# Attention's maxima by query tile and key tile for four heads at once, with the mask added by a 16-bit product

## The chip, the cores and the metric

The kernel runs on one core of a Trainium2 chip. Its engines are TensorE (PE; its weight loads are PEld in the profile), VectorE (DVE), ScalarE (ACT), GpSimd (POOL) and SyncE (SP), which issues most DMAs. The metric is the device time of one execution in microseconds (us), as the median of a few runs; lower is better.

## What is computed

Four steps one after the other on x of 4 x 1024 tokens x 128 numbers, each added to x behind a normalisation: attention, an expert layer, a message step, the expert layer again. The change is in the attention, which for 16 heads of 8 numbers is this:

```python
k = _layernorm((x @ Wk).reshape(b, t, h, s), kln_w, kln_b)   # q the same way
v = (x @ Wv).reshape(b, t, h, s)
dot = jnp.einsum('bqhs,bkhs->bhqk', q, k) * scale
dot = jnp.where(causal, dot, -jnp.inf)          # a query sees keys up to itself
attn = jax.nn.softmax(dot, axis=-1)
out = jnp.einsum('bhqk,bkhs->bqhs', attn, v).reshape(b, t, e)
return out @ Wo + bo
```

## The kernel before

A batch's 1024 tokens are 8 tiles of 128 (P). Heads go in groups of four (GROUP), four groups a batch, 16 groups in all. A head's 8 numbers are stacked to 32 rows (exact parts of both factors, and two rows for the shift), so that four heads fill 128 rows. `k_apart` holds the keys of a group with each head's 32 rows in a slab of its own and zeros elsewhere, so one product of all 128 rows gives one head's scores.

The softmax needs each query's largest allowed score first. So each group's scores are made twice:

- **Maxima.** Queries on the partitions, keys along the columns: `matmul(out, qT tile, k_apart[:, head, keys])` (L706), read by VectorE from PSUM. The causal mask matters only in the last 128 columns of a query tile's keys. VectorE adds a mask and takes the maximum in one fused instruction (L1239; the profile names it CUSTOM_DVE_ANT_0, and a short DVE_READ_ACCUMULATOR2_ANT brings its result), which writes the masked scores to a scratch tile. Where a row of keys has more than 512 columns, its first 512 are below the diagonal and take a plain reduction (L1237) into `first_max`.
- **Shift.** `shift` (L1244) takes the maxima of a half (four query tiles) with the sign turned into two spare rows of the stacked queries, `q_st`: for the high half joined with `first_max` first (L1250), then L1251 and L1252. TensorE transposes the queries again (`turn_shifted`, L710), into `qmT`, and the second scores come out less the maximum.
- **Scores.** Keys on the partitions, queries along the columns (L719). ScalarE takes the exponential out of PSUM into `a_prob` (L903), GpSimd clears what lies above the diagonal, and `weigh` (L723, its matmuls L739) multiplies by the values, four heads side by side in the array.

Work goes by **units**: one unit is one of six PSUM banks of 512 columns (`a_bank`, RINGS = 6), filled by TensorE and emptied by one other engine. TensorE fills unit n when unit n - 6 has been emptied, whoever empties it. Before, a maxima unit is one head's piece of the table MAX_PIECES: per head two units of 128 + 256 columns, two of 384 and six of 512, 40 a group.

The order is one generator, `sequence`, that all engines walk. It runs over the 40 score units of a group; behind score i stands the share of the 40 maxima units of the **next** group that are due by i (of 38 slots, i = 0 to 37), and at fixed i stand transposes, projections, normalisations and the weighs: behind 5 (key tiles 6 and 7 of the group before), 15, 20, 27, 32, 36 and 39. `turn_low`, which needs the low half's shift, is at 21; the shift of the high half at 37, and `turn_high` at 3 of the next group. So a group's maxima are made beside the scores of the group before, 15 times; the first group's are made alone, in the opening. Units with a diagonal tile are DVE's L1239; `spread` (SyncE's DMAs) lays out the keys, and KEYS_FROM says which maxima unit first reads their low and high half.

The causal mask `mask` is 128 x 512 in 16 bits, zero but for the last 128 columns, made by GpSimd in the setup.

## Time and profile before

| | us |
|---|---|
| median of 3 runs | 2802.59 (2801.55 to 2805.32) |
| the profiled execution | 2805.4 |
| its span | 2803.6 |
| mean granted TensorE clock | 0.972 of 2.4 GHz |
| attention with its opening | about the first 680 |
| expert layer, message step, expert layer | the rest |

The profile is of one execution. A row of the timeline is start, length, engine, line, operation, and tiles as output<-inputs; matmuls overlap, and their ends are modelled, so what a product costs TensorE in a stream is the distance between two starts. "PEld a <- DVE b: us, times" is TensorE's load for a that waited for VectorE's b. In rows of stretches each engine has its busy time with its count of instructions in brackets, then the granted clock (1.00 is 2.4 GHz), and DMA.

### The profile page before, as it was taken

How to read it: one execution, taken by the hardware profiler on the slowest of the kernel's cores; microseconds unless marked ns; L12 is line 12 of the kernel's file. 1: busy time of each engine (PE TensorE's matmuls, PEld its weight loads, DVE VectorE, ACT ScalarE, POOL GpSimd, SP SyncE). 2: the span in 40 equal slices, each digit the busy share in tenths (PEclk: the TensorE clock that was granted, in tenths of full speed). 3: DMA queues.
4: the chain of work that ended last, by engine and by line, in shares of the span. 5: the costliest groups of instructions: out<-in, count | busy, mean ns of one | idle time of the engine just before them, and what ended most of it. 6: DMA issues, size and time to landing. Idle time of an engine off the chain costs nothing. (4 is left out here: it accounts for less than half of the span.)

```text
span 2803.6 us, 54930 instructions
## 1 busy us (share of the span) xinstructions
PE 2600.8 (93%) x18814; PEld 1690.2 (60%) x18814; DVE 1769.6 (63%) x4095; ACT 1594.4 (57%) x2912; POOL 821.7 (29%) x1181
## 2 busy tenths in 40 slices
PE   6999999986689889999999999999999999996897
PEld 4566565653578755555556666555555565554786
DVE  7877777783656655556655556555566655546466
ACT  2776677775534455555555556665565555544343
POOL 4152524335154311111111111122121233313542
PEclk7999999998999899999999999999999999998998
DMA  5500000002334278888888888887888788874222
GB/s 110 87 16 12 16 16 16 13 19 83 96 113 135 66 176 198 195 195 200 193 197 195 196 195 192 195 187 186 191 192 194 187 204 204 205 183 178 60 84 86
DMA packets 193508, 383.24 MB, mean 137 GB/s; under 512 B 46305, under 2 KB 101738, under 8 KB 191882
## 3 DMA queue, kind: packets, MB, share of 16 engines
q1 hardware_dynamic: 184650, 362.55, 54.1%
q0 software_dynamic: 8640, 17.84, 1.8%
q8 instruction: 129, 2.11, 0.3%
q14 instruction: 89, 0.73, 0.1%
HBM read 38.10 MB, written 39.86 MB: 28 GB/s over the span
## 5 line engine op out<-in xcount | busy, mean ns | idle before, releaser
L3123 DVE STREAM_TRANSPOSE m_turned<-m_sig 128x1024 f32<-128x1024 f32 x512 | 613.7, 1228 | 419.8 <-ACT m_sig L2893 203.4
L2715 PE MATMUL m_v_ps<-m_sig,m_tok 128*64 128x512 f32 x2048 | 467.7, 598 | 0.0
L2728 PE MATMUL m_v_ps<-m_sigT,m_tok 128*64 128x256 f32 x4064 | 461.5, 380 | 2.9 <-DMA m_sigT<-m_turned 2.9
L2699 PE MATMUL m_f_ps<-m_swap,m_own 64*128 64x512 f32 x1536 | 424.7, 403 | 10.9 <-DMA m_swap<-m_own 8.1
L2699 PE MATMUL m_f_ps<-m_own,m_swap 64*128 64x512 f32 x1536 | 424.8, 403 | 0.0
L903 ACT ACTIVATE a_prob<-a_bank 128x512 f32<-128x512 f32 (+1 forms) x640 | 329.0, 567 | 167.7 <-PE a_bank L719 162.8
L2728 PEld LDWEIGHTS m_v_ps<-m_sigT,m_tok 128*64 128x64 f32 x4064 | 289.5, 137 | 197.9 <-issue 56.2
L2893 ACT ACTIVATE m_sig<-m_f_ps 128x1024 f32<-128x1024 f32 x256 | 248.4, 1023 | 236.3 <-issue 138.8
L2989 POOL TENSOR_TENSOR m_own<-m_uv,m_own 128x1024 fp32r<-128x1024 f32 x64 | 151.9, 2373 | 765.7 <-ACT m_own L2855 765.7
L2699 PEld LDWEIGHTS m_f_ps<-m_swap,m_own 64*128 64x128 f32 x1536 | 270.8, 186 | 93.4 <-issue 24.6
L2715 PEld LDWEIGHTS m_v_ps<-m_sig,m_tok 128*64 128x64 f32 x2048 | 135.6, 136 | 264.5 <-issue 264.1
L2879 ACT ACTIVATE m_sig<-m_f_ps 128x512 f32<-128x512 f32 x512 | 264.5, 603 | 45.7 <-PE m_f_ps L2699 44.0
L719 PE MATMUL a_bank<-a_qmT,k_apart 128*128 128x512 f32 (+3 forms) x768 | 265.8, 383 | 22.5 <-DVE a_maxima L1239 10.9
L706 PE MATMUL a_bank<-k_apart,a_qT 128*128 128x512 f32 (+3 forms) x768 | 265.2, 389 | 13.4 <-DVE a_maxima L1239 5.2
L2699 PEld LDWEIGHTS m_f_ps<-m_own,m_swap 64*128 64x128 f32 x1536 | 270.6, 186 | 5.2
L1239 DVE CUSTOM_DVE_ANT_0 a_masked_out<-a_bank,mask 128x128 f32<-128x128 f32 (+3 forms) x512 | 222.9, 485 | 54.3 <-PE a_bank L706 52.9
L719 PEld LDWEIGHTS a_bank<-a_qmT,k_apart 128*128 128x128 f32 x768 | 140.1, 193 | 132.5 <-issue 61.3
L2905 ACT CAST m_v1T_hi<-m_v_ps 128x256 fp32r<-128x256 f32 x128 | 47.8, 373 | 271.3 <-PE m_v_ps L2728 266.7
L1237 DVE TENSOR_REDUCE a_first_max<-a_bank 128x1 f32<-128x512 f32 x256 | 165.2, 684 | 49.6 <-PE a_bank L706 47.7
L3132 DVE TENSOR_TENSOR m_v1T_lo<-m_v_ps,m_v1T_hi 128x256 fp32r<-128x256 f32 x128 | 54.3, 424 | 201.6 <-ACT m_v1T_hi L2905 201.6
L706 PEld LDWEIGHTS a_bank<-k_apart,a_qT 128*128 128x128 f32 x768 | 144.1, 197 | 52.6 <-DVE a_maxima L1239 21.9
L1899 PE MATMUL f_y_ps<-f_w_down,f_innerT 128*128 x1136 | 153.4, 278 | 22.9 <-DVE f_raw L2309 15.7
(509 smaller groups left out, 4315.3 us busy)
## 6 DMA issues: line engine op xcount, KB each, us to landing
m_sigT<-m_turned SPq DMA_DIRECT2D x2042, 128.0 KB, 2.3
m_swap<-m_own SPq DMA_DIRECT2D x64, 256.0 KB, 3.3
f_t_rows<-f_sent_rows SPq DMA_DIRECT2D x142, 65.0 KB
f_sent_rows<-a_proj SPq DMA_DIRECT2D x34, 260.0 KB, 8.9
k_apart<-a_kT SPq DMA_DIRECT2D x128, 64.0 KB, 2.0
m_swap<-m_own SPq DMA_DIRECT2D x64, 128.0 KB, 3.2
f_h<-back_rows SPq DMA_DIRECT2D x8, 512.0 KB, 5.1
rows<-back_rows SPq DMA_DIRECT2D x6, 512.0 KB, 3.8
```

Source lines behind the costliest of these rows:

```text
L706: mm = pe.matmul(out[:, col:col + k1 - k0], qT[G % 2][:, qt * P:(qt + 1) * P], k_apart[G % 2][:, h, k0:k1], start=True, stop=True)
L719: mm = pe.matmul(out[:, col:col + q1 - q0], k_apart[G % 2][:, h, j * P:(j + 1) * P], qmT[G % 2][:, q0:q1], start=True, stop=True)
L903: act.activation(to[:, h, start:start + width], src[:, 0:width], ACT.Exp).then_inc(u.free(), 1)
L1237: ins = dve.tensor_reduce(first_max[:, qt % HALF_T, h:h + 1], scores, AX.X, ALU.max)
L1239: ins = dve.tensor_tensor_reduce(out=masked, in0=scores, in1=k["mask"][:, HALF - width:HALF], scale=1.0, scalar=MASKED, op0=ALU.add, op1=A ...
L1899: mm = pe.matmul(y_ps[:, 0:DIM], innerT[p][:, ib * P:(ib + 1) * P], w_down[:, ds(e * INTER + ib * DIM, DIM)], start=(ib == 0), stop=(ib == ...
L2699: mm = pe.matmul(f_ps[s][:, cols], tile_of(u[rows, :], j + s * SIDE), v[rows, cols], start=start, stop=stop)
L2715: mm = pe.matmul(v2_ps[h * RANK:(h + 1) * RANK, :], tok[p][:, 0, j + s * SIDE, :], sig[j % 2][s][:, h * HALF:(h + 1) * HALF], start=(j == ...
L2728: mm = pe.matmul(v1_ps[h * RANK:(h + 1) * RANK, g * 2 * P:(g + 1) * 2 * P], tok[p][:, 1, jj, :], sigT[g][:, :, 2 * h:2 * h + 2, jj, :].rea ...
L2879: ins = act.activation(sig[1][s][:, cols], f_ps[s][:, cols], ACT.Sigmoid)
L2893: act.activation(sig[j % 2][s][:, :], f_ps[s][:, :], ACT.Sigmoid).then_inc(sig_ready, 1)
L3123: dve.transpose(turned[g][:, :, q, :, :], sig[j % 2][s][:, :].rearrange("p (t j a) -> p j t a", j=4, a=STACK)).then_inc(turn_ready, 1)
```

## The change

A maxima unit is now one query tile by one key tile for all four heads: 128 columns for each head, 512 in all. There are 36 such pairs on and below the diagonal; the first, of query tile 0, is split into two units of two heads, so a group has 37 units. They stand in the order: query tiles 0 to 3 with their key tiles (11 units, and then the low shift), tiles 4 to 7 by key tiles 0 to 3 (16), tiles 4 to 7 by the high key tiles up to their own (10). Behind the product of a diagonal pair TensorE adds the mask into the same bank: a second product with a 16-bit identity as weights and the 128 x 128 mask, repeated for the heads, as the moving side. VectorE takes one plain reduction from 512 columns to 4 maxima (`maxima` for key tile 0, `tile_max` for the others); the fused instruction and its scratch tiles are gone. `shift` joins the key tiles' maxima with one small step for each key tile from 1 on: three for the low half, seven for the high one, each waiting for the one before it.

```diff
@@ setup, GpSimd
-            pool.wait_ge(ident_zero, 2)
+            pool.memset(k["ident16"][:, :], 0.0).then_inc(ident_zero, 1)
+            pool.wait_ge(ident_zero, 3)
+            pool.affine_select(out=k["ident16"][:, :], in_=k["ident16"][:, :], compare_op=ALU.not_equal, fill=1.0,
+                               base=0, pattern=[[-1, P]], channel_multiplier=1).then_inc(ident16_done, 1)
-            corner = k["mask"][:, HALF - P:HALF]
+            corner = k["mask"][:, :]
@@ attention, tables
-    SCORE_UNITS, MAX_UNITS = 40, 40
+    SCORE_UNITS, MAX_UNITS = 40, 37
-        MAX_PIECES = (((0, 0, P), (1, 0, 2 * P)), ((2, 0, 3 * P),), ((3, 0, HALF),), ((4, 0, HALF),), ((5, 0, HALF),),
-                      ((4, HALF, 5 * P), (5, HALF, 6 * P)), ((6, 0, HALF),), ((6, HALF, 7 * P),), ((7, 0, HALF),), ((7, HALF, SEQ),))
-        MAXES = [(pieces, (h + GROUP // 2) % GROUP) for pieces in MAX_PIECES for h in range(GROUP)]
+        MAXES = [(0, 0, 0, 2), (0, 0, 2, 2)]
+        MAXES += [(qt, kt, 0, GROUP) for qt in range(1, HALF_T) for kt in range(qt + 1)]
+        MAXES += [(qt, kt, 0, GROUP) for qt in range(HALF_T, TILES) for kt in range(HALF_T)]
+        MAXES += [(qt, kt, 0, GROUP) for qt in range(HALF_T, TILES) for kt in range(HALF_T, qt + 1)]
-        KEYS_FROM = (0, 20)
-        MAXES_LOW = 12
+        KEYS_FROM = (0, 27)
+        MAXES_LOW = 11
@@ TensorE, maxima_unit
-                for qt, k0, k1 in pieces:
-                    mm = pe.matmul(out[:, col:col + k1 - k0], qT[G % 2][:, qt * P:(qt + 1) * P], k_apart[G % 2][:, h, k0:k1], start=True, stop=True)
-                    col += k1 - k0
+                to = out[:, 0:heads * P].rearrange("p (h k) -> p h k", h=heads)
+                mm = pe.matmul(to, qT[G % 2][:, qt * P:(qt + 1) * P], k_apart[G % 2][:, h:h + heads, kt * P:(kt + 1) * P], start=True, stop=kt < qt)
+                if kt == qt:
+                    mm = pe.matmul(to, k["ident16"][:, :], k["mask"][:, :].unsqueeze(1).broadcast_to([P, heads, P]), start=False, stop=True)
@@ VectorE, maxima_unit
-                for qt, k0, k1 in pieces:
...
-                        ins = dve.tensor_reduce(first_max[:, qt % HALF_T, h:h + 1], scores, AX.X, ALU.max)
-                        continue
-                    ins = dve.tensor_tensor_reduce(out=masked, in0=scores, in1=k["mask"][:, HALF - width:HALF], scale=1.0,
-                                                   scalar=MASKED, op0=ALU.add, op1=ALU.max, accum_out=maxima[:, qt, h:h + 1])
+                at = maxima[:, qt, h:h + heads] if kt == 0 else tile_max[:, qt, kt - 1, h:h + heads]
+                ins = dve.tensor_reduce(at, src[:, 0:heads * P].rearrange("p (h k) -> p h k", h=heads), AX.X, ALU.max)
@@ VectorE, shift
-                if n:
-                    link(dve.tensor_tensor(maxima[:, mine, :], maxima[:, mine, :], first_max[:, :, :], ALU.max))
+                for kt in range(1, (n + 1) * HALF_T):
+                    upper = slice(max(kt, mine.start), mine.stop)
+                    link(dve.tensor_tensor(maxima[:, upper, :], maxima[:, upper, :], tile_max[:, upper, kt - 1, :], ALU.max))
```

TensorE's program in batch 0, group 3, from score 28 to the weigh behind score 32 (L719 is a score, L706 a maxima product, L671 a transpose, L739 a weigh). Before:

```order
L719 MATMUL a_bank<-a_qmT,k_apart 128x512
L706 MATMUL a_bank<-k_apart,a_qT 128x384
L719 MATMUL a_bank<-a_qmT,k_apart 128x512
L706 MATMUL a_bank<-k_apart,a_qT 128x384
L719 MATMUL a_bank<-a_qmT,k_apart 128x512
L706 MATMUL a_bank<-k_apart,a_qT 128x512
L719 MATMUL a_bank<-a_qmT,k_apart 128x512
L671 MATMUL a_bank<-ident,k_st 128x128 x4
L706 MATMUL a_bank<-k_apart,a_qT 128x512
L719 MATMUL a_bank<-a_qmT,k_apart 128x384
L706 MATMUL a_bank<-k_apart,a_qT 128x512
L739 MATMUL a_o_acc<-a_prob,v 32x128 x4
```

The same place now, from the maxima product behind score 28 to the last instruction ahead of that weigh; L723 is a score, L709 a maxima product, L711 the mask's product, L674 a transpose:

```order
L709 MATMUL a_bank<-k_apart,a_qT 128x512
L723 MATMUL a_bank<-a_qmT,k_apart 128x512
L709 MATMUL a_bank<-k_apart,a_qT 128x512
L711 MATMUL a_bank<-mask,ident 128x512
L723 MATMUL a_bank<-a_qmT,k_apart 128x512
L709 MATMUL a_bank<-k_apart,a_qT 128x512
L723 MATMUL a_bank<-a_qmT,k_apart 128x512
L674 MATMUL a_bank<-ident,k_st 128x128 x4
L709 MATMUL a_bank<-k_apart,a_qT 128x512
L723 MATMUL a_bank<-a_qmT,k_apart 128x384
L709 MATMUL a_bank<-k_apart,a_qT 128x512
L711 MATMUL a_bank<-mask,ident 128x512
```

The maxima products are all 512 wide, and a mask product stands behind two of them, one of the two right ahead of the weigh.

VectorE at the shift of a high half, before; the ISA rows are the fused reduction and its short second instruction:

```order
L1239 ISA a_masked_out,a_maxima<-a_bank,mask 128x512 [waits a_unit_free4,a_unit_full]
L1239 ISA a_maxima 128x1
L1239 ISA a_masked_out,a_maxima<-a_bank,mask 128x512 [waits a_unit_free1,a_unit_full]
L1239 ISA a_maxima 128x1
L1250 TENSOR_TENSOR a_maxima<-a_maxima,a_first_max 128x16 [waits a_unit_free5]
L1251 TENSOR_SCALAR q_st<-a_maxima 128x4x4 [waits a_link]
L1252 SCALAR_TENSOR_TENSOR q_st<-a_maxima,q_st 128x4x4 [waits a_link]
```

And now:

```order
L1231 TENSOR_REDUCE a_tile_max<-a_bank 128x4 [waits a_unit_full] x13
L1241 TENSOR_TENSOR a_maxima<-a_maxima,a_tile_max 128x16 [waits a_unit_free4]
L1241 TENSOR_TENSOR a_maxima<-a_maxima,a_tile_max 128x16 [waits a_link] x3
L1241 TENSOR_TENSOR a_maxima<-a_maxima,a_tile_max 128x12 [waits a_link]
L1241 TENSOR_TENSOR a_maxima<-a_maxima,a_tile_max 128x8 [waits a_link]
L1241 TENSOR_TENSOR a_maxima<-a_maxima,a_tile_max 128x4 [waits a_link]
L1243 TENSOR_SCALAR q_st<-a_maxima 128x4x4 [waits a_link]
L1244 SCALAR_TENSOR_TENSOR q_st<-a_maxima,q_st 128x4x4 [waits a_link]
```

One join has become seven, each waiting for the last.

## Rows read from the trace of the kernel before

**Rows 1.** The page, part 1: busy us (share) x instructions of each engine.
```profile
PE 2600.8 (93%) x18814; PEld 1690.2 (60%) x18814; DVE 1769.6 (63%) x4095; ACT 1594.4 (57%) x2912; POOL 821.7 (29%) x1181
```

**Rows 2.** Engines' busy time in stretches S2, S5, S7 of a group, and all seven's sum.
```profile
core 0: us, PE busy (x) PEld busy (x) DVE busy (x) ACT busy (x) POOL busy (x), PEclk, DMA share, GB/s
...
187.65:195.77 8.12, 7.78 (x42) 3.91 (x38) 7.02 (x19) 5.88 (x11) 3.75 (x9) 1.00 0.00 0
...
206.99:210.99 4.00, 4.00 (x34) 2.53 (x30) 2.94 (x7) 2.94 (x6) 0.78 (x2) 1.00 0.23 51
...
214.75:216.60 1.85, 1.85 (x20) 1.10 (x16) 1.01 (x4) 1.33 (x3) 0.00 (x0) 1.00 0.00 0
sum 33.25, PE 32.91 PEld 20.71 DVE 25.68 ACT 23.46 POOL 9.13; mean PE 4.70 PEld 2.96 DVE 3.67 ACT 3.35 POOL 1.30
```

**Rows 3.** TensorE in order of time in that group: start, length, instruction.
```profile
183.69 0.62 PE L706 MATMUL a_bank<-k_apart,a_qT 128*128 128x128 f32 x4
184.15 0.40 PE L719 MATMUL a_bank<-a_qmT,k_apart 128*128 128x512 f32 x1
...
188.47 0.40 PE L706 MATMUL a_bank<-k_apart,a_qT 128*128 128x512 f32 x1
188.70 0.40 PE L719 MATMUL a_bank<-a_qmT,k_apart 128*128 128x512 f32 x1
...
193.91 1.92 PE L739 MATMUL a_o_acc<-a_prob,v 128*32 128x512 f32 x16
...
208.60 0.60 PE L671 MATMUL a_bank<-ident,k_st 128*128 128x128 f32 x4
208.96 0.48 PE L706 MATMUL a_bank<-k_apart,a_qT 128*128 128x512 f32 x1
209.28 0.34 PE L719 MATMUL a_bank<-a_qmT,k_apart 128*128 128x384 f32 x1
209.45 0.40 PE L706 MATMUL a_bank<-k_apart,a_qT 128*128 128x512 f32 x1
209.78 1.28 PE L739 MATMUL a_o_acc<-a_prob,v 128*32 128x128 f32 x16
```

**Rows 4.** VectorE in order of time in the opening, columns as in rows 3.
```profile
54.75 0.28 DVE L1239 CUSTOM_DVE_ANT_0 a_masked_out<-a_bank,mask 128x128 f32<-128x128 f32 x1
...
55.30 0.29 DVE L1239 CUSTOM_DVE_ANT_0 a_masked_out<-a_bank,mask 128x128 f32<-128x128 f32 x1
...
60.79 0.55 DVE L1239 CUSTOM_DVE_ANT_0 a_masked_out<-a_bank,mask 128x384 f32<-128x384 f32 x1
...
61.27 2.48 DVE L1237 TENSOR_REDUCE a_first_max<-a_bank 128x1 f32<-128x512 f32 x4
63.66 0.68 DVE L1239 CUSTOM_DVE_ANT_0 a_masked_out<-a_bank,mask 128x512 f32<-128x512 f32 x1
...
64.27 0.68 DVE L1239 CUSTOM_DVE_ANT_0 a_masked_out<-a_bank,mask 128x512 f32<-128x512 f32 x1
...
66.22 0.17 DVE L1250 TENSOR_TENSOR a_maxima<-a_maxima,a_first_max 128x16 f32<-128x16 f32 x1
66.43 0.18 DVE L1251 TENSOR_SCALAR q_st<-a_maxima 128x16 fp32r<-128x16 f32 x1
```

**Rows 5.** Waits over 150 to 650 us: us in total, times, longest; first and last of eight.
```profile
PEld a_bank L719 <- DVE a_maxima L1239: 24.2, 40, 2.5
...
PE a_bank L706 <- DVE a_first_max L1237: 1.0, 4, 0.3
```

**Rows 6.** Groups of instructions by form, and one line's durations (min/median/max).
```profile
L739 PE MATMUL a_o_acc<-a_prob,v 128*32 128x512 f32 x768 | 99.2, 604 | 5.5 <-POOL a_prob L1049 4.1 <-ACT a_prob L903 1.4
...
L1237 DVE TENSOR_REDUCE a_first_max<-a_bank 128x1 f32<-128x512 f32 x256 | 165.2, 684 | 49.6 <-PE a_bank L706 47.7
...
L1172 DVE TENSOR_REDUCE a_qk_var<-a_spare x8: 895/1204/1218, 35.8 to 448.9; 128x128 f32<-128x1024 f32 x6, 128x96 f32<-128x768 f32 x2
```

**Rows 7.** Engines' busy time in the opening's maxima, columns as in rows 2.
```profile
42.50:66.80 24.30, 20.54 (x50) 12.41 (x49) 24.13 (x85) 0.59 (x1) 14.72 (x20) 0.62 1.20 189
```

More of the change, by code:

```diff
@@ L344, in attention_phase @@
     HEAD_STAGES, EARLY_UNITS = 5, 12
-    MASKED_OUTS = 2
     with ExitStack() as ctx, ExitStack() as phase:
@@ L368, in attention_phase @@
         qT, kT, qmT = ([sb(f"a_{n}{i}", [P, SEQ], F32R) for i in range(c)] for n, c in (("qT", 2), ("kT", 1), ("qmT", 2)))
-        maxima, first_max = sb("a_maxima", [P, TILES, GROUP]), sb("a_first_max", [P, HALF_T, GROUP])
-        masked_out = [sb(f"a_masked_out{i}", [P, HALF]) for i in range(MASKED_OUTS)]
+        maxima, tile_max = sb("a_maxima", [P, TILES, GROUP]), sb("a_tile_max", [P, TILES, TILES - 1, GROUP])
         oT = sb("a_oT", [P, SEQ])
@@ L699, in maxima_unit @@
             def maxima_unit(u, G, n, stacks=()):
-                pieces, h = MAXES[n]
-                out, col = u.next(), 0
+                qt, kt, h, heads = MAXES[n]
+                out = u.next()
                 u.wait_empty(pe, *stacks)
@@ L1220, in stack_first, with maxima_unit @@
                 dve.memset(qs[:, :, :, 3 * HD:3 * HD + 2], 0.0).then_inc(queries_ready, 1)
[L1222 to L1224 removed]
+            def maxima_unit(u, n):
+                qt, kt, h, heads = MAXES[n]
+                src = u.next()
                 u.wait_full(dve)
[L1226 to L1240 removed]
+                at = maxima[:, qt, h:h + heads] if kt == 0 else tile_max[:, qt, kt - 1, h:h + heads]
+                ins = dve.tensor_reduce(at, src[:, 0:heads * P].rearrange("p (h k) -> p h k", h=heads), AX.X, ALU.max)
                 ins.then_inc(u.free(), 1)
@@ L1443, in early_table, with group @@
                 dve.tensor_scalar(k["early_expert"][:, :], expert_sum[0:1, :], -1.0, None, ALU.add)
-            def group(u, link, b, g, prev, prep, follows, masked_by, head_made=()):
+            def group(u, link, b, g, prev, prep, follows, head_made=()):
                 ahead, projected = (g + 1) % GROUPS, []
@@ L1449, in group @@
                     if what == "max":
-                        made = maxima_unit(u, n, masked_by)
+                        made = maxima_unit(u, n)
                     elif what == "next_keys":
@@ L1531, in _ @@
             u.n += 4
-            masked_by = []
             for what, n in opening():
                 if what == "max":
-                    made = maxima_unit(u, n, masked_by)
+                    made = maxima_unit(u, n)
                 elif what == "shift":
@@ L1540, in _ @@
             u.next()
-            group(u, link, 0, 0, False, False, True, masked_by)
+            group(u, link, 0, 0, False, False, True)
             before, made = link.n, ()
@@ L1545, in _ @@
                 for g in (1, 2, 3):
-                    made = group(u, link, b, g, True, True, True, masked_by, made)
-                made = group(u, link, b + 1, 0, True, True, True, masked_by, made)
-                masked_by = [n - UNITS_BATCH for n in masked_by]
+                    made = group(u, link, b, g, True, True, True, made)
+                made = group(u, link, b + 1, 0, True, True, True, made)
                 before += link.n
@@ L1553, in _ @@
             for g in (1, 2, 3):
-                made = group(u, link, b, g, True, False, g < GROUPS - 1, masked_by, made)
+                made = group(u, link, b, g, True, False, g < GROUPS - 1, made)
             for n in range(HALVES_OF):
@@ L3401, in hybrid_kernel @@
         with ExitStack() as attention:
-            allocate(attention, k, {"mask": ([P, HALF], BF16),
+            allocate(attention, k, {"mask": ([P, P], BF16), "ident16": ([P, P], BF16),
                                     "w_qkv": ([P, 3 * DIM], F32), "w_o": ([P, DIM], F32),
```

14 lines of the change are left out of this document (1 added, 13 removed).

## The prediction

> **What bounds the kernel now.** I read the page first [rows 1]: TensorE is busy 93% of the span, VectorE 63%, ScalarE 57%. The change touches attention alone, which fills about the first 680 us, so the whole-span shares decide nothing. I then took one steady group (batch 0, group 3), from 183.35 to 216.60 us, and cut it at the ends of its products with the probabilities (weigh) into seven stretches, S1 to S7 [rows 2]. The reader should see in the sum TensorE at 32.91 us of 33.25, VectorE at 25.68, ScalarE at 23.46: three engines that share a ring of six PSUM banks, at full clock. A busy TensorE is not one at its peak, because ends of matmuls are modelled, so I went down to start-to-start times.
>
> Paces on TensorE [rows 3]: 512-column products start 0.232 us apart (188.47, 188.70), a 384-column one takes 0.175 (209.28 to 209.45), and two units of 128 plus 256 columns fill 183.69 to 184.15, 0.23 each. Transposes of four tiles take 0.36 (208.60 to 208.96), and the 512-column product right behind them 0.32 (208.96 to 209.28), 0.09 more than in the stream. Paces on VectorE [rows 4]: masked reduction of 512 columns 0.61 us, of 384 0.48, a pair 128 plus 256 0.555 (54.75, 55.30); four plain reductions of 512 take 2.39, so 0.598 each; a small step on the maxima 0.21.
>
> With these, S5 is 5 scores (4 x 0.232 + 0.175 = 1.10), 5 maxima units (3 x 0.232 + 2 x 0.175 = 1.05), one transposing unit 0.36 and weigh 1.21: 3.72 of its 4.00 us. The other 0.28 is what TensorE loses behind transposes and on either side of a weigh, 0.09 to 0.1 each (the weigh starts at 209.78, 0.33 after a product that wants 0.23 [rows 3]). So S5 is TensorE's, and so by the same count are S1, S3, S4, S6 and S7 (VectorE is busy 2.94 of 4.00 us in S5 [rows 2]). S2 is different: 10 scores 2.21, 11 units 2.44, weigh 1.9 (its row at 193.91 [rows 3]) make 6.5 of 8.12 us, and VectorE is busy for 7.02: VectorE sets that stretch by giving banks back late. Over 150 to 650 us TensorE's loads and matmuls of scores and maxima wait for VectorE's maxima in eight rows, from 24.2 down to 1.0 us, together 65 [rows 5].
>
> **The change part by part.** Maxima of a group are made 16 times: once in the opening, alone, and 15 times between the scores of the group before.
>
> TensorE, columns. Before, per group: 4 heads x (2 x 0.23 + 2 x 0.175 + 6 x 0.232) = 8.8 us. Now 35 units of 512 columns and 2 of 256 (two in 0.23): 8.35 us. Saved 0.4 us. The columns multiplied are the same; only the narrow pieces, which cost more per column, are gone.
>
> TensorE, masks. New are 9 identity products in 16 bits, 7 of 512 columns and 2 of 256. No row before has a 16-bit product. The nearest are products of the same shape in the same stream, 0.232 per 512 [rows 3]. Below: the weigh products, which run for four heads at once, 99.2 us for 768, 0.13 each [rows 6]. Above: the transposes, products with an identity too, 0.36 for 4 x 128 columns [rows 3]. I take 0.232, the row of equal shape: 8 x 0.232 = 1.86 us a group; the ends give 1.0 and 2.9.
> The Trainium skill (TensorE: Matmul & The Clock Gate, Back-to-back issue gap) states about 131 ns a matmul of 512 columns in a sustained stream of loads and matmuls. Rows 3 disagree with that (0.23); by it the masks would cost 8 x 0.131 = 1.05 us, and the sum below would be some 12 us smaller.
>
> Net on TensorE +1.4 us a group. Where it falls, with the units moved from 40 over 38 scores to 37 over 37: S1 +0.13, S2 +0.58 (two masks; the narrow units leave), S3 -0.23 (5 units for 6), S4 +0.35 (the mask of unit 27 and wider units), S5 +0.57 (masks of 29 and 32), S6 +0.23 (mask of 36), S7 -0.23 (no unit left). In S1 and S3 to S7 this is on the path: +0.82.
>
> VectorE, units. Before 4 x (2 x 0.555 + 2 x 0.48 + 6 x 0.61) = 22.9 us, now 35 x 0.598 + 2 x 0.35 = 21.6: it saves 1.3. This supposes that a reduction to four values costs what one to a single value does. The reduction of 1024 columns to 128 values lasts 1204 ns against 684 for 512 to one [rows 6]: 520 ns for 512 more columns, so outputs cost nothing; without that row 35 x 0.1 us would be at stake.
> The Trainium skill (VectorE: DVE Perf Modes, Rules for kernel authors) speaks against the change: `tensor_reduce` is "the slowest DVE op", to be restructured away. Rows 4 do not bear that out here (0.598 us between starts against 0.61 for the fused one); by the rule the units would cost more and the slower end of my range would be the likely one.
>
> VectorE, joins. The shift of the low half gets three more small steps, that of the high half six more: 9 x 0.21 = 1.9 us. The high ones run in S7, where VectorE has been idle beside the weighs (it is busy 1.01 of 1.85 us [rows 2]), and the transposes that need them come three scores into the next group; the last unit is now two scores earlier. They cost nothing there; without the cover 1.3 us a group. What is queued behind them is the next group's first unit, whose bank is needed six units later. The low ones run in S2, where VectorE sets the pace. S1 and S2 together on VectorE: units 9.63 to 9.07 us, shift +0.63, net +0.07. TensorE wants +0.58 in S2 and has 1.6 us of waits there to put it in. Bounds 0.07 and 0.58; I take 0.3, between, because a weigh needs the units before it issued, not averaged.
>
> Sum per group 0.82 + 0.3 = 1.12, times 15 = 16.8 us.
>
> Opening (42.5 to 66.8, VectorE busy 24.13 of 24.30 us, mean granted clock 0.62 [rows 7]). VectorE bounds it: 24.3 us before; now 21.6 of units, 1.5 for the low shift (0.89 + 0.63) and 2.0 for the high one (0.73 + 1.26): 25.1, +0.8. TensorE is mostly at its lower level there (1.2 GHz); twice 0.232 us, an estimate, for each of the last ten units and four masks is 6.5 us against VectorE's 6.0. The ring hides part of it; without that cover +0.5. Setup: GpSimd's 16-bit identity adds a memset and a selection, and the mask's memset shrinks to a quarter; VectorE waits for x, not for them. Nothing.
>
> Against the profiled run's own 2805.4 us the sum is +17.6: 2823.0. That run is 2.8 us over the median of 2802.6, so the forecast of the median is 2820. SyncE's spreads are not moved; the high keys are now first read at unit 27, not 20, later and not sooner.
>
> **Rivals.** A, slower by masks on the path: the sum above, 2820 (2811 to 2831).
> B, masks absorbed: TensorE's slack takes them. If the 0.28 us left in S5, and the like 0.56 in S4 and 0.36 in S6, could be filled, 1.2 us of a group's gain in work vanishes and 2803 to 2808 comes out. For it: waits for banks of 65 us. Against it: S5's slack is accounted for by what follows transposes and weighs, which a mask doesn't fill.
> C, masks dearer: 0.36 a mask instead of 0.232 adds 8 x 0.13 x 15 = 15 us: 2835; a loss of 0.09 us behind each 16-bit product, as behind transposes, adds 10 x 0.09 x 15 = 13: 2834; both, 2848.
> D, faster: VectorE's returning of banks, not TensorE, sets all stretches. Then each stretch goes by VectorE's own change: S1 -0.7, S2 +0.13, S3 -0.5, S4 +0.2, S5 +0.2, S6 -0.05, S7 -0.6 with the joins in idle time: -1.3 a group, 2784. It decides if TensorE's waits for banks in S3 to S7 are real and over 1 us a group. For it: the same 65 us. Against: VectorE is idle over 1 us of each stretch but S2.
> E, the change doesn't do what it says (units or masks other than 37 and 9 on the chip): its order lists them, so next to nothing.
>
> **Chances and range.** A 0.53, B 0.20, C 0.14, D 0.12, E 0.01. A measurement of this kernel can tell about 0.2%, 5.6 us, from no change. D alone is faster by over that (0.12); B lies mostly within it (0.20); A and C are slower (0.68). The range 2796 to 2842 takes in A, B, most of C and the edge of D.
>
> **What would show it.** Mask products with starts 0.23 us behind their unit's product: cost right. Reductions 0.6 us apart: VectorE right. S5's counterpart at 4.5 us or more and S3's at 5.1: the distribution. Group 3 at about 34.4 us for 33.25. An opening of 25 us. If a mask's start-to-start is 0.13, or a weigh starts no later after its last unit than before, the forecast is too high; if scores wait for VectorE's maxima less than before and S3 to S7 shrink, D is true. Reductions over 0.65 us apart would prove the four outputs dear and the forecast low.

## The result and the profile after

| | before | after |
|---|---|---|
| median | 2803.95 (4 runs, 2801.55 to 2806.04) | 2854.46 (4 runs, 2853.52 to 2857.36) |
| ratio | | 1.0177 [1.0165, 1.019] |
| span of the profiled execution | 2803.6 | 2855.6 |
| attention with its opening (end of the last weigh) | 675.49 | 726.23 |
| all behind it | 2128.1 | 2129.3 |

The change makes the kernel 1.8% slower, 50.5 us where the forecast had 17.6, and outside its range. Nearly all of it is in attention, which ends 50.7 us later. The page of after, part 1:

```profile
PE 2623.6 (92%) x18782; PEld 1679.2 (59%) x18782; DVE 1806.3 (63%) x3551; ACT 1594.5 (56%) x2912; POOL 820.9 (29%) x1183
```

Against [rows 1] TensorE is busy 23 us more and VectorE 37, with 544 instructions fewer. The span is 52 us longer, so TensorE also stands idle for 29 us more: the loss is more waiting, and not only more work. The group of the forecast, by the same cuts as [rows 2] (first to last column: length, busy time of each engine with its count, granted clock, DMA):

```profile
core 0: us, PE busy (x) PEld busy (x) DVE busy (x) ACT busy (x) POOL busy (x), PEclk, DMA share, GB/s
...
203.31:212.91 9.60, 8.08 (x44) 4.12 (x40) 8.37 (x17) 6.00 (x11) 3.71 (x9) 1.00 0.01 2
...
224.19:228.77 4.58, 4.58 (x36) 2.68 (x32) 3.31 (x5) 3.05 (x6) 0.78 (x2) 1.00 0.20 44
...
232.76:234.38 1.62, 1.62 (x19) 0.92 (x15) 1.34 (x9) 1.14 (x3) 0.00 (x0) 1.00 0.00 0
sum 35.19, PE 33.67 PEld 20.07 DVE 27.15 ACT 23.50 POOL 9.09; mean PE 4.81 PEld 2.87 DVE 3.88 ACT 3.36 POOL 1.30
```

S5 is 0.58 longer than before and S7 0.23 shorter, as forecast. S2 has grown by 1.48 us, and VectorE is busy in it for 8.37 us, not 7.02. But this group costs 1.94 us; fifteen like it would be 29. Cutting all of attention at each group's first score shows where the others are. The columns are the group whose scores are made, its length in us, and the difference; groups 2, 6 and 10 (group 2 of a batch) are those beside whose scores VectorE and GpSimd normalise the heads of the next batch.

| stretch | before | after | difference |
|---|---|---|---|
| opening, up to the first score | 67.30 | 70.79 | +3.5 |
| group 2 | 37.06 | 47.25 | +10.2 |
| group 6 | 38.03 | 47.07 | +9.0 |
| group 10 | 37.26 | 46.97 | +9.7 |
| the other 13, together | 495.8 | 514.2 | +18.3 |

More than half of the loss is in three groups that the forecast had taken to be like group 3. In group 2, VectorE, then GpSimd and then TensorE in order of time (start, length, engine, line, operation):

```profile
165.24 1.21 DVE L1231 TENSOR_REDUCE a_tile_max<-a_bank 128x4 f32<-128x512 f32 x2
166.49 3.35 DVE L1241 TENSOR_TENSOR a_maxima<-a_maxima,a_tile_max 128x12 f32<-128x12 f32 x3
169.87 0.18 DVE L1243 TENSOR_SCALAR q_st<-a_maxima 128x16 fp32r<-128x16 f32 x1
170.09 2.20 DVE L1244 SCALAR_TENSOR_TENSOR q_st<-a_maxima,q_st 128x16 fp32r<-128x16 f32 x1
172.21 0.68 DVE L1231 TENSOR_REDUCE a_maxima<-a_bank 128x4 f32<-128x512 f32 x1
```
```profile
165.40 1.97 POOL L1020 TENSOR_TENSOR a_qk<-a_qk,a_spare 128x1024 f32<-128x1024 f32 x1 [2.81 <-DVE a_spare L1182]
167.45 4.79 POOL L1024 TENSOR_TENSOR a_qk<-a_qk,ln_rows 128x1024 f32<-128x1024 f32 x2
```
```profile
172.94 0.79 PE L709 MATMUL a_bank<-k_apart,a_qT 128*128 128x512 f32 x1 [4.64 <-DVE a_maxima L1231]
```

Three joins of 12, 8 and 4 numbers last 3.35 us together, though a free one takes 0.17. One by one they last 0.911, 0.166 and 2.207 us, from 166.486 on. The first ends 0.03 us behind GpSimd's L1020, the third 0.02 behind the first of the two L1024; then L1244, started right into the second L1024, lasts 2.20 and ends 0.04 behind it. I call such a step held: it has started, and doesn't end before GpSimd's instruction does. From the first join to VectorE's next reduction 5.7 us pass. ScalarE empties its banks meanwhile, but VectorE gives none back; TensorE fills the banks in order, and stands still for 4.64 us at the first one that VectorE has still to empty.

Over the whole trace, with the start of each step set against GpSimd's instructions: 105 joins that start beside none last 171 ns in the median (at most 176), 55 that start beside one last 486 (at most 2210), 31.4 us in all, of which some 22 are waiting. Of these 55, 39 are held and last 300 ns or more. The other 16 last as long as free ones: nine of them start in the last 0.12 us of GpSimd's instruction, and seven beside its DMA_INDIRECT (it issues transfers for the expert layer), which holds none.

```profile
L1241 DVE TENSOR_TENSOR a_maxima<-a_maxima,a_tile_max x160: 152/174/2210, 49.7 to 693.8; 128x16 f32<-128x16 f32 x64, 128x12 f32<-128x12 f32 x32, 128x8 f32<-128x8 f32 x32, 128x4 f32<-128x4 f32 x32
```
```profile
692.55 1.40 DVE L1241 TENSOR_TENSOR a_maxima<-a_maxima,a_tile_max 128x16 f32<-128x16 f32 x7
```
```profile
692.38 0.99 POOL L1085 DMA_INDIRECT f_sent_rows<-a_spare,early_rows  x1 [0.17 <-issue]
```

The trace of before had the holding too, in a row that I hadn't looked at: the first of the shift's two last steps, beside GpSimd's L1016.

```profile
157.61 0.90 DVE L1251 TENSOR_SCALAR q_st<-a_maxima 128x16 fp32r<-128x16 f32 x1
```
```profile
156.49 1.98 POOL L1016 TENSOR_TENSOR a_qk<-a_qk,a_spare 128x1024 f32<-128x1024 f32 x1 [2.72 <-DVE a_spare L1178]
```

The step ends at 158.51, GpSimd's at 158.47. The forecast took its 0.18 us from the row at 66.43 in [rows 4], where GpSimd runs nothing.

The masks, the largest term in the forecast, are where it put them. TensorE beside the scores of group 0:

```profile
78.84 0.39 PE L709 MATMUL a_bank<-k_apart,a_qT 128*128 128x512 f32 x1
79.07 0.39 PE L711 MATMUL a_bank<-mask,ident 128*128 128x512 bf16 x1
79.11 0.58 PE L723 MATMUL a_bank<-a_qmT,k_apart 128*128 128x512 f32 x1
79.53 0.39 PE L709 MATMUL a_bank<-k_apart,a_qT 128*128 128x512 f32 x1
```

From the mask's start at 79.07 to the next unit's at 79.53 there are 0.46 us for a mask and a score, 0.23 each. The score's start in between is the records' model. VectorE in the opening:

```profile
60.24 7.85 DVE L1231 TENSOR_REDUCE a_tile_max<-a_bank 128x4 f32<-128x512 f32 x13
68.12 1.41 DVE L1241 TENSOR_TENSOR a_maxima<-a_maxima,a_tile_max 128x16 f32<-128x16 f32 x7
```

Units of four maxima are 0.60 us apart (7.85 for 13), as those of one were: here three more outputs cost nothing, as supposed.

### The profile page after: what moved, and what is told of

It is laid out like the page before. It is cut to its first block and busy times, and to the rows that moved or that the text cites. A ratio compares the mean times of both kernels' runs of the same rounds, so it can differ in the third digit from the quotient of the medians.

```text
span 2855.6 us, 53950 instructions
## 1 busy us (share of the span) xinstructions
PE 2623.6 (92%) x18782; PEld 1679.2 (59%) x18782; DVE 1806.3 (63%) x3551; ACT 1594.5 (56%) x2912; POOL 820.9 (29%) x1183
## 5 line engine op out<-in xcount | busy, mean ns | idle before, releaser
L1231 DVE TENSOR_REDUCE a_tile_max<-a_bank 128x4 f32<-128x512 f32 x448 | 292.3, 683 | 106.0 <-PE a_bank L709 92.3
L709 PE MATMUL a_bank<-k_apart,a_qT 128*128 128x512 f32 (+1 forms) x592 | 256.2, 441 | 34.4 <-DVE a_maxima L1231 24.9
L723 PE MATMUL a_bank<-a_qmT,k_apart 128*128 128x512 f32 (+3 forms) x768 | 274.0, 397 | 14.8 <-ACT a_prob L907 8.3
L723 PEld LDWEIGHTS a_bank<-a_qmT,k_apart 128*128 128x128 f32 x768 | 139.1, 194 | 121.1 <-issue 68.4
L743 PE MATMUL a_o_acc<-a_prob,v 128*32 128x512 f32 (+3 forms) x1536 | 156.4, 520 | 8.0 <-issue 5.4
L709 PEld LDWEIGHTS a_bank<-k_apart,a_qT 128*128 128x128 f32 x592 | 116.4, 197 | 74.5 <-DVE a_maxima L1231 33.4
```

The lines of the kernel that those rows point to most:

```text
L709: mm = pe.matmul(to, qT[G % 2][:, qt * P:(qt + 1) * P], k_apart[G % 2][:, h:h + heads, kt * P:(kt + 1) * P], start=True, stop=kt < qt)
L723: mm = pe.matmul(out[:, col:col + q1 - q0], k_apart[G % 2][:, h, j * P:(j + 1) * P], qmT[G % 2][:, q0:q1], start=True, stop=True)
L743: mm = pe.matmul(o_acc[h * STACK:(h + 1) * STACK, q0:q1], v1[:, j, g * GROUP + h, :], weights_at[:, h, q0 - off:q1 - off], start=(j == 0), ...
L1231: ins = dve.tensor_reduce(at, src[:, 0:heads * P].rearrange("p (h k) -> p h k", h=heads), AX.X, ALU.max)
```

## The experiments

Two explanations stood against each other. By the first, from the trace, the joins make the loss, by their number and by being held until a GpSimd instruction in flight has ended. By the second, the forecast's own (rival A, dearer than it was priced), the masks on TensorE's path make it. Ratios are to the kernel before, run on the same chip; the lengths of attention and of its stretches are those of the profiled executions. In what was expected of the first four runs, theory P stands for the first explanation and theory M for the second; later ones say what theirs are.

### One reduction for all the joins: one_join

```diff
-                for kt in range(1, (n + 1) * HALF_T):
-                    upper = slice(max(kt, mine.start), mine.stop)
-                    link(dve.tensor_tensor(maxima[:, upper, :], maxima[:, upper, :], tile_max[:, upper, kt - 1, :], ALU.max))
+                made_by = tile_max[:, mine, 0:(n + 1) * HALF_T, :].rearrange("p q k g -> p q g k")
+                link(dve.tensor_reduce(maxima[:, mine, :], made_by, AX.X, ALU.max))
```

All maxima go to `tile_max` here, whose unused places hold the masked value from the start.

> The changed kernel with its joins made otherwise: key tile maxima are kept side by side (unused places hold -1e30), and each shift joins them with one reduction of one operand instead of three or seven small two-operand steps that wait for each other. Masks, units and order stay. Theory P (each two-operand or scalar step on operands in SBUF waits until the GpSimd instruction in flight has ended; in the group that follows the head normalisation the three low steps lasted 3.35 us and the two behind them 2.4, beside GpSimd instructions of 2 to 2.4 us): a reduction isn't held, the three slow groups lose most of their 9 to 10 us, the others about 1: 2816 to 2828. Theory M (the mask products on TensorE cost three times what they were priced at): nothing much changes, 2845 to 2855.

Measured: 2807.65 us, 0.9995 [0.9985, 1.0004]. That is below the range of either theory: the joins cost more than P had put down to them. Attention ends at 675.51 us, for 726.23 of after and 675.49 of before. So another way of joining gives back the whole 50.7 us: 4.9 in the opening, 29.0 in groups 2, 6 and 10, and 16.8 in the others. VectorE and GpSimd at the low shift of group 6:

```profile
305.55 0.27 DVE L1240 TENSOR_REDUCE a_maxima<-a_tile_max 128x16 f32<-128x64 f32 x1
305.85 0.63 DVE L1242 TENSOR_SCALAR q_st<-a_maxima 128x16 fp32r<-128x16 f32 x1
306.51 0.19 DVE L1243 SCALAR_TENSOR_TENSOR q_st<-a_maxima,q_st 128x16 fp32r<-128x16 f32 x1
306.62 2.56 DVE L1231 TENSOR_REDUCE a_tile_max<-a_bank 128x4 f32<-128x512 f32 x4
```
```profile
304.46 1.98 POOL L1020 TENSOR_TENSOR a_qk<-a_qk,a_spare 128x1024 f32<-128x1024 f32 x1 [2.82 <-DVE a_spare L1182]
306.52 4.88 POOL L1024 TENSOR_TENSOR a_qk<-a_qk,ln_rows 128x1024 f32<-128x1024 f32 x2
```

The reduction runs its 0.27 us in the middle of L1020. The step behind it is held until 306.48, GpSimd's end at 306.44; the last one starts 0.01 us ahead of the next GpSimd instruction and isn't. From the join to the next reduction on the maxima 1.07 us pass, and the banks move on.

### The masks left out: no_mask, one_join_no_mask

```diff
-                mm = pe.matmul(to, ..., start=True, stop=kt < qt)
-                if kt == qt:
-                    mm = pe.matmul(to, k["ident16"][:, :], k["mask"][:, :].unsqueeze(1).broadcast_to([P, heads, P]), start=False, stop=True)
+                mm = pe.matmul(to, ..., start=True, stop=True)
```

Both leave the causal mask out of the maxima (the probabilities are still cleared above the diagonal): no_mask in the kernel after, one_join_no_mask in one_join.

> The changed kernel without the masks' products (left out: the causal mask in the maxima; the maxima then run over keys beyond the diagonal too). Theory P: masks cost what they were priced at, 8 x 0.232 us x 15 at most, partly hidden: 10 to 25 us less than 2854, so 2830 to 2845. Theory M: 40 us and more less, 2815 or below.

> The changed kernel with one reduction as the join, and without the masks' products (left out: the causal mask in the maxima). If masks cost by themselves what the stretches S4 to S6 of the other run without them show (0.9 us a group) and joins add on top: 2807 less 13 to 20: 2787 to 2795. If the masks only cost where joins had filled the ring: 2802 to 2808.

Measured: no_mask 2840.55, 1.0114 [1.0097, 1.0131], attention 19.0 us shorter than after's; one_join_no_mask 2796.07, 0.9945 [0.9928, 0.9961], attention 12.3 us shorter than one_join's. The first lies in P's range; the second is 1 us above its first range and far from the other. So the masks cost 12 us of attention where no chain of joins is in the way, and the second explanation can't carry 50. In group 3 no_mask takes 0.23 us from S4, 0.48 from S5 and 0.23 from S6: one, two and one mask's worth by the forecast's price.

### The joins alone, held and not held: before_joins, before_reduces

The kernel before, with as many steps more in each shift as after has (three low, six high), chained as there. In before_joins they are of two operands, in before_reduces reductions of one, each of a single number per output (its loop is the same). The first kind joins every value with itself, the second writes to a tile that nothing reads.

```diff
+                for kt in range(1 + n, (n + 1) * HALF_T):
+                    upper = slice(max(kt, mine.start), mine.stop)
+                    link(dve.tensor_tensor(maxima[:, upper, :], maxima[:, upper, :], maxima[:, upper, :], ALU.max))
```
```diff
+                    link(dve.tensor_reduce(same_max[:, upper, :], maxima[:, upper, :].unsqueeze(3), AX.X, ALU.max))
```

> The kernel before with the changed one's small steps added and nothing else: three two-operand steps more at the low shift, six at the high one, of the same sizes, each the maximum of the maxima with themselves, chained by waits. Theory P: most of the loss appears here: 2825 to 2842, with 6 to 9 us in each of the three groups behind the head normalisation. Theory M: 9 x 0.21 us, mostly in idle time: 2804 to 2812.

> As the kernel before with nine chained steps added, but each a reduction of one operand of the same size into a scratch tile instead of a two-operand step. Theory P (the kind of step is held by GpSimd, not the count): 2804 to 2812. A rival, that nine chained waits are themselves the cost: the same as with the two-operand steps, 2825 and more.

Measured: before_joins 2876.15, 1.0231 [1.0214, 1.0248], attention +65.5 us; before_reduces 2841.84, 1.0113 [1.0096, 1.013], attention +32.0. Both missed P's range: the first is 34 us above it, and the second is neither at P's 2804 to 2812 nor, as its rival had it, as slow as the first. The added instructions of each over the whole trace (min/median/max in ns):

```profile
L1253 DVE TENSOR_TENSOR a_maxima<-a_maxima x144: 161/176/2220, 49.1 to 709.5; 128x16 f32<-128x16 f32 x48, 128x12 f32<-128x12 f32 x32, 128x8 f32<-128x8 f32 x32, 128x4 f32<-128x4 f32 x32
```
```profile
L1254 DVE TENSOR_REDUCE a_same_max<-a_maxima x144: 157/166/171, 49.2 to 675.4; 128x16 f32<-128x16 f32 x48, 128x12 f32<-128x12 f32 x32, 128x8 f32<-128x8 f32 x32, 128x4 f32<-128x4 f32 x32
```

97 of these reductions start beside a GpSimd instruction (five of them beside its DMA_INDIRECT), and none lasts over 171 ns; steps of two operands of the same size last up to 2220. The low shift of group 2 in before_joins and, behind it, in before_reduces:

```profile
168.94 3.34 DVE L1253 TENSOR_TENSOR a_maxima<-a_maxima 128x12 f32<-128x12 f32 x3
172.31 0.18 DVE L1254 TENSOR_SCALAR q_st<-a_maxima 128x16 fp32r<-128x16 f32 x1
172.53 2.20 DVE L1255 SCALAR_TENSOR_TENSOR q_st<-a_maxima,q_st 128x16 fp32r<-128x16 f32 x1
```
```profile
166.41 0.55 DVE L1254 TENSOR_REDUCE a_same_max<-a_maxima 128x12 f32<-128x12 f32 x3
167.00 0.31 DVE L1255 TENSOR_SCALAR q_st<-a_maxima 128x16 fp32r<-128x16 f32 x1
167.34 0.19 DVE L1256 SCALAR_TENSOR_TENSOR q_st<-a_maxima,q_st 128x16 fp32r<-128x16 f32 x1
```
```profile
165.29 1.97 POOL L1017 TENSOR_TENSOR a_qk<-a_qk,a_spare 128x1024 f32<-128x1024 f32 x1 [2.72 <-DVE a_spare L1179]
```

The last row is GpSimd's in before_reduces: the three reductions pass beside it, the TENSOR_SCALAR behind them waits for its end at 167.26. So about half of what nine such steps cost is the kind that is held (33.5 us), and half comes with steps of the other kind too (32.0). Nine steps of 0.21 us in 16 groups are 30 us, as much as if each of them were on the path. But it isn't their number alone: the two steps behind them, which can be held, last 22.5 us in all in before_reduces and 17.8 in before. How the 32 us divide between the two isn't shown.

The Trainium skill (SBUF — State Buffer, Who interferes with whom) says that a VectorE instruction with two SBUF inputs contends with a GpSimd instruction that reads SBUF, and so does one in a two-port mode, which `tensor_scalar` can enter, where whoever issues first has the shared pair of ports for the whole instruction; on trn2 a `tensor_reduce` never contends. The traces here agree, with the durations above. By its other clause two SBUF inputs don't collide with a GpSimd instruction that only writes. The traces agree with that too, in the setup of every run; in before, VectorE and GpSimd:

```profile
7.27 0.17 DVE L88 TENSOR_TENSOR a_spread<-a_stats 128x8 f32<-128x8 f32 x1
7.48 0.17 DVE L89 SCALAR_TENSOR_TENSOR a_spread<-a_spread,a_work 128x8 f32<-128x8 f32 x1
7.68 0.82 DVE L90 TENSOR_SCALAR a_mean<-a_mean 128x8 f32<-128x8 f32 x1
```
```profile
4.96 3.52 POOL L258 MEMSET k_apart<- 128x4096 f32 x1
```

Five steps of two operands, from 6.66 us on, take 0.17 us each in the middle of a clearing of 3.52 us. The TENSOR_SCALAR behind them takes 0.82 and ends at 8.50 us, 0.02 behind the clearing's end. So what holds depends on both instructions: a GpSimd instruction that only writes held the TENSOR_SCALAR and not the joins' kind.

### The shift without held steps, the units spread wider: all_reduce, spread39, before_shift_reduced

all_reduce is one_join with the shift's two steps as reductions as well, four in place of three instructions (the diff is against one_join); before_shift_reduced does the same to the kernel before; spread39 is all_reduce with the maxima units due by score 39, not 37.

```diff
-                link(dve.tensor_reduce(maxima[:, mine, :], made_by, AX.X, ALU.max))
+                dve.tensor_reduce(both[:, mine, :, 0], made_by, AX.X, ALU.max, negate=True)
+                dve.tensor_reduce(both[:, mine, :, 1].bitcast(F32R), made_by, AX.X, ALU.max)
...
-                link(dve.tensor_scalar(hi.bitcast(F32R), maxima[:, mine, :], -1.0, None, ALU.mult))
-                dve.scalar_tensor_tensor(out=lo.bitcast(F32R), in0=maxima[:, mine, :], scalar=-1.0, in1=hi,
-                                         op0=ALU.mult, op1=ALU.subtract).then_inc(shift_ready, 1)
+                link(dve.tensor_reduce(hi.bitcast(F32R), made_by, AX.X, ALU.max, negate=True))
+                with nc.allow_low_precision(reason="two parts of one number, exact"):
+                    dve.tensor_reduce(lo.bitcast(F32R), both[:, mine, :, :], AX.X, ALU.add).then_inc(shift_ready, 1)
```

> One reduction as the join, and the two steps of the shift behind it made by reductions too (the negated maximum rounded, the plain one rounded, the negated one, and their sum as the remainder): three unchained and one chained step, none of the kinds that GpSimd holds. Theory P: it gains what the two held steps lose, 0.2 to 0.5 us a shift near GpSimd's work, less two more steps of 0.2 us: 2800 to 2808, and no small VectorE step beside GpSimd's work lasts over 0.3 us. Rival (count of steps decides): 2810 to 2818.

> The kernel before with the two steps of its shift that GpSimd can hold made by reductions (three unchained and one chained). Theory P: it gets back what held steps lost in the kernel before, some 6 us in all by its trace, less two more steps of 0.17 us in each of 32 shifts where VectorE is late: 0.997 to 1.0. If being held cost nothing here (it sits in idle time), two more steps cost: 1.0 to 1.003.

> The same as the kernel with the whole shift in reductions, and the 37 units spread over all 40 scores of a group instead of 38, so that S7, where VectorE idles, gets a unit and S2, where VectorE sets the pace, loses about a half. Theory (S2 is VectorE's, the others TensorE's): 0.3 to 0.6 us a group less in S2, 4 to 9 us in all: 2794 to 2802. Rival: the high shift now ends too late for its transposes at score 3, and S1 grows by as much or more: 2805 to 2820.

Measured: all_reduce 2810.59, 0.9999 [0.9989, 1.0008]; before_shift_reduced 2810.59, 1.0002 [0.9993, 1.0012]; spread39 2812.22, 1.0004 [0.9994, 1.0014]. all_reduce and spread39 missed theory P's ranges and came out in their rivals'; before_shift_reduced lies where the two of its expectations meet. No step of all_reduce's shift lasts over 397 ns, which is the length of a reduction of the high half's maxima and no waiting, and S2 of group 3 falls from 9.02 to 8.68 us. But there is more work elsewhere: the steps of all shifts sum up to 36.6 us, for 30.6 in one_join, and the opening is 1.8 us longer. Attention ends 0.4 us earlier. Two steps a shift that can be held are no loss worth this change. In group 3 the wider spread moved 0.4 us out of S2 and 0.5 out of S4 and put 0.7 into S7; S1, where the rival had put the loss, stayed as it was.

### The head normalisation moved away from the joins: after_late

```diff
-                    yield {5: ("square_sums", 0), 7: ("head_dev", 0), 8: ("head_rstd", 1), 9: ("affine", 1), 12: ("stack_keys", 0),
...
+                    yield {5: ("square_sums", 0), 7: ("head_dev", 0), 10: ("head_rstd", 1), 11: ("affine", 1), 12: ("stack_keys", 0),
...
```

The kernel after, with GpSimd's long instructions (L1020, L1024) two scores later, behind the low shift.

> The changed kernel, joins and masks as they are, with one thing moved in the group behind the head normalisation: VectorE's reciprocal that releases GpSimd's long instructions (2.0, 2.4 and 2.4 us) goes from behind score 8 to score 10, behind the low shift, and GpSimd's part from 9 to 11. So the low joins meet no long GpSimd instruction. Theory P (a small step waits out the GpSimd instruction in flight): S2 of groups 2, 6 and 10 falls from 17.6 us to 12 to 14, the whole to 2838 to 2846. Rival (the joins cost through their chain alone, wherever they stand): S2 stays near 17 and the whole near 2854.

Measured: 2838.25, 1.0092 [1.0075, 1.0109], as theory P expected. By the ratios it is 0.85% better than after, some 24 us, with attention 19.9 us shorter, by a move of two table entries. S2 of group 6 falls from 17.63 to 11.14 us (12 to 14 were expected), and groups 2, 6 and 10 from 47 to 40.6, 39.0 and 40.6: six to eight us each come from where the joins meet GpSimd. The number of joins is the same, so this part is the holding and not the count.

### The masks moved into the stretch with slack: masks_early and its variants

What still makes S4 to S6 of one_join longer than before's is the masks, 0.23 us each. masks_early is one_join with the four high diagonal units right behind the low shift, in S2, where TensorE waits anyway. masks_early_late has after_late's move too, masks_early_39 the spread to score 39.

```diff
-        MAXES += [(qt, kt, 0, GROUP) for qt in range(HALF_T, TILES) for kt in range(HALF_T)]
-        MAXES += [(qt, kt, 0, GROUP) for qt in range(HALF_T, TILES) for kt in range(HALF_T, qt + 1)]
+        MAXES += [(qt, qt, 0, GROUP) for qt in range(HALF_T, TILES)]
+        MAXES += [(qt, kt, 0, GROUP) for qt in range(HALF_T, TILES) for kt in range(qt)]
...
-        KEYS_FROM = (0, 27)
+        KEYS_FROM = (0, 11)
```

> The changed kernel with one reduction as the join, and the four diagonal units of the high half, with their masks, moved from the stretches S4 to S6, where TensorE sets the pace, to right behind the low shift, into S2, where VectorE does. Theory (a mask costs 0.23 us where TensorE is the bound and next to nothing where it waits for banks): S4, S5 and S6 fall by 0.23, 0.46 and 0.23 us, S2 stays at 9.0 to 9.3: 8 to 13 us less than the same kernel with the masks late, 0.995 to 0.997 of before. Rival (a mask costs its 0.23 us anywhere): the same as with the masks late, 0.9985 to 1.0005.

> The same, and the reciprocal that releases GpSimd's long instructions moved behind the low shift in the group behind the head normalisation. Theory P: two held steps in three groups, 0.5 us a group and what follows from them: 1 to 4 us less than without it. If GpSimd's later end delays the stacked keys, up to 5 us more.

> The same as the last, with the 37 units over all 40 scores. It took 0.3 us from S2 and 0.46 from S4 before but gave 0.7 back in S7: within 3 us of the last, either way.

Measured: masks_early 2815.14, 1.0021 [1.0011, 1.003], above both of its ranges; masks_early_late 2814.43, 1.0019 [1.0009, 1.0028], no different from it by what the measurement can tell (its attention is 1.6 us shorter); masks_early_39 2824.24, 1.005 [1.0036, 1.0064], 10 us from masks_early_late where at most 3 were expected. Yet groups 3 to 10 had each become shorter than one_join's, by 0.7 to 2.4 us. One group had not: group 1, at 55.05 us for 41.02. Waits of masks_early in it (us, times, longest), and SyncE's queue:

```profile
PE a_bank L709 <- DMA k_apart<-a_kT: 11.8, 1, 11.8
```
```profile
108.35 9.72 SPq L612 DMA_DIRECT2D f_sent_rows<-a_proj  x6
118.17 3.18 SPq L622 DMA_DIRECT2D k_apart<-a_kT  x4
```

The new order reads group 2's high keys at unit 11, and their spread stands in SyncE's queue behind transfers of 260 KB that clear buffers for the expert layer. In one_join they landed at 120.2 us and were first read by unit 27 at 131.4; here TensorE is ready for unit 11 at 115.0 us, they land at 126.6, and it waits 11.8 us, once. The part of the plan that was moved had a second need, and the forecast of it looked only at the engines. masks_early_39's profiled run (2816.6 us) is faster than its other four (2822 to 2826) and its attention ends where masks_early's does, so its trace doesn't show why the others are slower, which stays open.

### The same without that wait: masks_early_but_one

For group 2 alone the order and the wait are after's; all others are as in masks_early. masks_early_but_one_reduce has all_reduce's shift too, masks_early_but_one_late after_late's move.

```diff
+        KEYS_LATE = MAXES + [(qt, kt, 0, GROUP) for qt in range(HALF_T, TILES) for kt in range(HALF_T)]
+        KEYS_LATE += [(qt, kt, 0, GROUP) for qt in range(HALF_T, TILES) for kt in range(HALF_T, qt + 1)]
...
-                qt, kt, h, heads = MAXES[n]
+                qt, kt, h, heads = (KEYS_LATE if G == 2 else MAXES)[n]
...
+                keys_from = (0, 27) if G == 2 else KEYS_FROM
```

> masks_early, with the diagonal units of batch 0, group 2 alone (made beside the scores of group 1) back behind its low key tiles, so that its high keys are first read at unit 27. In masks_early's trace TensorE waited once for them, 11.78 us at 114.99, ahead of that group's unit 11, behind 17 transfers of 260 KB on SyncE's queue, and group 1 took 55.05 us for one_join's 41.02; groups 3 to 10 took 0.6 to 2.4 us less each than in one_join. Theory P (masks on TensorE's path are worth 0.2 us each and the rest of masks_early was this one wait): group 1 back at 41 to 42 us, attention ends at 668 to 670 us for before's 675.5, ratio 0.9965 to 0.9985. Rival R (the masks' time merely moves into S2, and a gain in groups 3 to 10 is given back): attention at 674 or later, ratio 0.999 to 1.001.

> masks_early_but_one, with the shift's two steps as reductions too, as in all_reduce: no step of two operands is left behind GpSimd's instructions, but there are two steps more. In all_reduce S2 of group 3 was 8.68 us for one_join's 9.02, and the opening 1.7 us longer. Theory P: within 2 us of masks_early_but_one, ratio 0.9955 to 0.9985. Rival R: as all_reduce, 1.000.

> masks_early_but_one, with the head normalisation's reciprocal and its affine step behind scores 10 and 11, not 8 and 9. That move took 16 us from the kernel after, whose held joins stood beside it, and 1.5 us of attention from masks_early. Theory P: with one join there is next to nothing left to free: within 2 us of masks_early_but_one, ratio 0.996 to 0.9985. Rival: groups 2, 6 and 10 fall by 1 us or more each, 3 us less than masks_early_but_one.

Measured: 2802.27, 0.998 [0.9971, 0.9989]; with reductions 2802.32, 0.9976 [0.9967, 0.9985]; with the move 2801.84, 0.9979 [0.997, 0.9988]. Group 1 is back at 41.23 us and attention ends at 668.9, 6.6 us ahead of before's. Group 3 of masks_early_but_one, S4 to S6 and the sum:

```profile
201.36:207.25 5.89, 5.89 (x43) 3.67 (x39) 4.47 (x7) 4.62 (x9) 0.00 (x0) 1.00 0.06 13
207.25:211.36 4.11, 4.11 (x35) 2.57 (x31) 3.11 (x5) 2.94 (x6) 0.78 (x2) 1.00 0.22 49
211.36:215.12 3.76, 3.76 (x30) 2.50 (x26) 2.58 (x5) 2.68 (x6) 0.78 (x2) 1.00 0.00 0
...
sum 33.80, PE 33.23 PEld 20.03 DVE 25.55 ACT 23.41 POOL 9.06; mean PE 4.75 PEld 2.86 DVE 3.65 ACT 3.34 POOL 1.29
```

S4, S5 and S6 were 6.13, 4.57 and 3.99 us in one_join: one, two and one masks less, and S2, which took them in, is 0.11 longer. This version keeps the mask and is faster than both kernels, than before by 0.2%, with an interval clear of 1, and than after by 2.0% (1.0177 over 0.998). All three came out within theory P's ranges, and neither variant differs from it by more than the measurement can tell, as was expected.

## Why the forecast went wrong

The step that failed is "VectorE, joins", in its price and in its claim of cover. It had nine small steps at 1.9 us of VectorE a group, of which the high ones were to cost nothing and the low ones a part of S2's 0.3 us. One reduction in the place of each chain gives back 50.7 us (one_join), where the whole forecast was 17.6.

- **Price of a join.** 0.21 us came from a row where GpSimd was idle. In after a join takes what that row shows in 121 cases of 160; 39 are held by a GpSimd instruction, for some 22 us in all. The question to ask of a price is what ran beside its row; [rows 1] alone says that GpSimd is busy 29% of the span.
- **Cover.** "They cost nothing there" was right for group 3, where S1 is 4.12 us in after and in one_join. In group 6 S1 is 7.98 us in after and 4.12 in one_join; the high joins ahead of it ran beside GpSimd's L1014, took 2.76 us for 1.41, and TensorE waited 2.10 us for a bank. The granted clock in after's S1 was 0.79, in one_join's 1.00, so that some of it is TensorE at a lower granted clock behind the waits; that part wasn't separated. And in the order of before, nine steps that nothing holds lengthen attention by 32 us, so idle time of VectorE in a stretch is no cover by itself.
- **S2.** Forecast +0.3 us with bounds up to 0.58, came +1.48. S1 and S2 together were forecast at +0.43; one_join has +0.72 and all_reduce, whose shift nothing holds, +0.38. That this comes near is in part luck: S1 was forecast at +0.13 and came at -0.18 in all three, and all_reduce's S2 is +0.56, close to the forecast's upper bound.
- **Masks and units.** S3 to S7 were forecast at -0.23, +0.35, +0.57, +0.23 and -0.23, and came at -0.22, +0.28, +0.58, +0.23 and -0.23. A mask costs 0.23 us, a reduction to four values 0.60. These steps held, within 0.07 us.
- **One group for fifteen.** Group 3's +1.12 was multiplied by 15. In one_join group 3 has +1.35, but the fifteen groups that have maxima beside them +3.1 together, and the last, which has none, -1.7; the opening has -1.4. Groups 1, 3, 4, 7 and 8 are 1.0 to 1.4 us longer, groups 0 and 12 0.9 to 1.1 shorter; what the others wait for in the place of the masks wasn't followed up. So the term of 16.8 us was too high by some 14 and hid as much of the joins' miss. That the total came out no further from the forecast is luck.
- **Opening.** +0.8 forecast, +3.5 came, and -1.4 in one_join. In after its three low joins took 2.23 us, for 0.6.
- **Rivals.** A was right in its direction and its mechanism (12 us of masks on the path), though not as the cause of the size. B's time came out in one_join, at 0.9995, but not by its mechanism: there the masks still cost 12 us, and other groups and the opening gain. C's dearer masks are refuted by the starts, D by S3 to S7. None named the joins, which carry the result.

The Trainium skill (VectorE: DVE Perf Modes, Rules for kernel authors) calls `tensor_reduce` "the slowest DVE op" and advises to consider restructuring. The traces here disagree: the units' reductions are 0.60 us apart for 0.61 of the fused instruction, and putting two reductions in the place of ten small `tensor_tensor` steps a group took 50.7 us off.

## What to carry to other kernels

The price of a chain of small VectorE steps depends on what GpSimd runs beside it: look at the longest duration of such a step in the trace, not at its median, and find what it ended with. Where several partial results are to be joined, store them side by side and take one reduction, which neither waits for GpSimd nor repeats a step's fixed cost. And before one group stands for all, cut every group once and see whether they are alike; before a unit is moved forward, look in the DMA queue for when its operand lands.

## What the runs showed of the hardware

- VectorE's small steps of two SBUF operands, and its TENSOR_SCALAR on SBUF operands, that started while a GpSimd instruction ran which reads SBUF mostly ended 0.01 to 0.05 us behind its end; one that takes 0.17 us alone lasted up to 2.22 (before_joins). Reductions, 97 of them beside GpSimd in before_reduces, took at most 171 ns.
- Beside a GpSimd MEMSET of 3.52 us the steps of two operands took 0.17 us, and the TENSOR_SCALAR ended with it (before, 6.66 to 8.50 us). Seven joins beside GpSimd's DMA_INDIRECT took 161 to 175 ns (after).
- This holds for short instructions of GpSimd too: one of its selections, of 0.64 us (L1049 in before_joins), made a join of 16 numbers last 0.55 us at 154.59.
- A product with a 16-bit identity as weights and a 16-bit mask of 512 columns takes 0.23 us in the stream, as one in 32 bits does; only its weight load is shorter (95 ns at the least in after, for 186).
- A reduction of 512 PSUM columns to four values lasts 683 ns in the mean (after), to one value 684 [rows 6].
